# Sixty-four attention heads on four engines: paired low parts, an earlier scaling, a subtraction moved to GpSimd, and a cell layer with six output banks

## What is computed

```python
y = x.reshape(b, t, 16, 8).transpose(0, 2, 1, 3)           # 16 heads of 8 features
scores = jnp.einsum('bhtk,bhsk->bhts', y, y) / math.sqrt(8)
attn = jax.nn.softmax(scores, axis=-1)
o = jnp.einsum('bhts,bsc->bhtc', attn, x)                  # values: all 128 features
return o.transpose(0, 2, 1, 3).reshape(b, t, 16 * c) @ weight
```

```python
def step(c, xt):
    ft = sigmoid(xt @ wf.T + c @ uf.T + bf); it = sigmoid(xt @ wi.T + c @ ui.T + bi)
    gt = tanh(xt @ wc.T + c @ uc.T + bc)
    return ft * c + it * gt, None
c_final, _ = lax.scan(step, c0, x)
h = tanh(einsum('tbi,oi->tbo', x, wo) + c_final @ uo.T + bo)
```

## Time and profile before

| | us |
|---|---|
| median of 3 runs | 2707.84 |
| profiled execution: its own time | 2715.62 |
| profiled execution: span | 2713.8 |
| head attention with its normalisation | about 612 to 1652 |
| cell0 and cell1, outputs only | about 2307 to 2319, and 2697 to 2711 |

### The profile page before, as it was taken

How to read it: one execution, slowest core, us unless ns; L and a number is a source line. 1 busy time by engine, 2 the same in 40 slices (tenths; PEclk the granted TensorE clock), 3 DMA queues, 4 the chain that set the end, 5 groups by cost and what they waited for, 6 DMA issues and landing times. The chain is left out here.

```text
span 2713.8 us, 34921 instructions
## 1 busy us (share of the span) xinstructions
PE 2542.2 (94%) x11075; PEld 1905.0 (70%) x11075; DVE 2209.5 (81%) x3128; ACT 1828.7 (67%) x3038; POOL 1227.6 (45%) x1258
## 2 busy tenths in 40 slices
PE   7899999996999999999999998899999999788888
PEld 4788888874666666666666665688888886467656
DVE  6687777777999999999999996787778875577665
ACT  4455555556888888888888885455555555566676
POOL 3566766664233233232332322466766663154411
PEclk9999999998999999999999999999999999788999
DMA  4566666644333333333333331566666650000000
GB/s 110 116 143 138 136 137 145 144 98 160 101 104 99 106 102 98 109 101 102 103 102 105 102 91 44 125 144 142 136 137 145 143 120 8 24 24 8 9 7 33
DMA packets 107384, 271.46 MB, mean 100 GB/s; under 512 B 30784, under 2 KB 35648, under 8 KB 107072
## 3 DMA queue, kind: packets, MB, share of 16 engines
q1 hardware_dynamic: 82192, 235.42, 35.4%
q0 software_dynamic: 24576, 33.62, 4.6%
q10 hardware_dynamic: 432, 0.20, 0.0%
HBM read 258.35 MB, written 10.76 MB: 99 GB/s over the span
## 5 line engine op out<-in xcount | busy, mean ns | idle before, releaser
L684 POOL TENSOR_TENSOR moe_experts_lo<-moe_experts_hidden,moe_experts_hi 128x512 fp32r<-128x512 f32 x512 | 662.4, 1294 | 340.5 <-ACT moe_experts_hi L622 340.3
L968 DVE TENSOR_TENSOR heads_e_lo<-heads_e,heads_e_hi 128x1024 fp32r<-128x1024 f32 x512 | 616.1, 1224 | 25.9
L629 ACT ACTIVATE psum<-psum 128x512 f32<-128x512 f32 x512 | 298.0, 582 | 478.6 <-PE psum L90 478.6
L802 POOL DMA_DIRECT2D heads_left<-heads_parts x512 | 307.5, 616 | 671.5 <-PE psum L856 610.3
L908 ACT ACTIVATE heads_e<-psum 128x1024 f32<-128x1024 f32 x512 | 520.8, 1024 | 108.0 <-PE psum L856 108.0
L656 DVE TENSOR_TENSOR moe_experts_weighted<-moe_spread,psum 128x512 f32<-128x512 f32 x512 | 351.3, 686 | 189.4 <-PE psum L90 185.7
L88 PE MATMUL psum<-heads_e_hi,heads_v_lo 128*128 128x512 f32 x1024 | 429.6, 420 | 18.3 <-DVE heads_u L934 18.3
L88 PE MATMUL psum<-moe_n_hi,moe_w_lo 128*128 128x512 f32 x1024 | 400.8, 391 | 5.6 <-PEq L54 5.4
L89 PE MATMUL psum<-heads_e_lo,heads_v_hi 128*128 128x512 f32 x1024 | 404.2, 395 | 0.0
L90 PE MATMUL psum<-heads_e_hi,heads_v_hi 128*128 128x512 f32 x1024 | 400.7, 391 | 0.0
L89 PE MATMUL psum<-moe_n_lo,moe_w_hi 128*128 128x512 f32 x1024 | 400.0, 391 | 0.0
(11 more groups left out here) (403 smaller groups left out, 4078.1 us busy)
## 6 DMA issues: line engine op xcount, KB each, us to landing
moe_spread<-moe_mask SPq DMA_DIRECT2D x128, 1024.0 KB, 10.2
heads_right<-heads_parts SPq DMA_DIRECT2D x512, 64.0 KB
heads_left<-heads_parts POOLq DMA_DIRECT2D x512, 64.0 KB, 2.5
heads_scale<-heads_inverse_copy SPq DMA_DIRECT2D x64, 512.0 KB, 3.7
moe_experts_raw<-in_gate SPq DMA_DIRECT2D x16, 256.0 KB, 11.7
moe_experts_raw<-in_up SPq DMA_DIRECT2D x16, 256.0 KB, 11.8
moe_experts_raw<-in_down SPq DMA_DIRECT2D x16, 256.0 KB, 11.7
heads_parts<-heads_e_hi SPq DMA_DIRECT2D x16, 256.0 KB, 3.2
```

The source lines that it names most:

```text
L629: act.activation(psum[:, GATE + p % 2, :], psum[:, GATE + p % 2, :], ACT.Silu).then_inc(silu_ready, 1)
L684: pool.tensor_tensor(lo[:, p, :], hidden[:, p % 2, :], f(hi[:, p, :]), ALU.subtract).then_inc(low_ready, 1)
L802: eng.dma_start(f(tile[row:row + 2 * HEAD, h % 2, :]), parts_dram[dims, order:order + 2, at]).then_inc(loaded[h % 2], 16)
L968: dve.tensor_tensor(e_lo[:, s, :], e[:, s % 4, :], f(e_hi[:, s, :]), ALU.subtract).then_inc(low, 1)
```

## The change

- **Low parts in pairs.** VectorE goes in steps of two key tiles: cast of the even tile, then one subtraction 128x2048 for both tiles, once both high parts are there. `low` counts pairs, and so do the waits of ScalarE (ring buffer free) and TensorE.
- **Scaling earlier.** `scale_sums` goes after the cast of tile 4 and ahead of the low parts of tiles 4 and 5 (before: after the low part of tile 5).
- **`invert` later.** It goes behind the cast of tile 0 (before: ahead of it).
- **`u_lows` on GpSimd**, ahead of the `heads_left` loads of three heads on.
- **Cells.** The eight outputs take turns in six banks, four of which hold gate sums until the last step's gates are taken; the `wo` products run four outputs ahead of the `uo` products.

```diff
@@ head_attention, gpsimd
+                def u_lows(g):
+                    for half in range(HALVES):
+                        pool.wait_ge(u_high, g * HALVES + half + 1)
+                        pool.tensor_tensor(u_lo[:, g % 2, half, :], u[:, half, :], f(u_hi[:, g % 2, half, :]),
+                                           ALU.subtract).then_inc(u_low, 1)
                 for h in range(2, COUNT):
+                    if h >= 3:
+                        u_lows(h - 3)
                     pool.wait_ge(scores_done, (h - 1) * TILES)
                     load_head(pool, left, (0, 0), h, left_loaded)
+                for g in range(COUNT - 3, COUNT):
+                    u_lows(g)
@@ tensor, scalar
-                    pe.wait_ge(low, h * TILES + s + 1)
+                    pe.wait_ge(low, (h * TILES + s) // 2 + 1)
-                    after(act, low, n - 3)
+                    after(act, low, n // 2 - 1)
@@ vector
-                for n in range(COUNT * TILES):
+                for n in range(0, COUNT * TILES, 2):
                     h, s = n // TILES, n % TILES
+                    dve.wait_ge(exp_done, n + 1)
+                    after(dve, out_done, n - (TILES - 1))
...
+                    dve.tensor_copy(e_hi[:, s, :], e[:, s % 4, :]).then_inc(dve_high, 1)
                     if s == 0 and h >= 1:
                         invert(h - 1)
...
-                    dve.tensor_tensor(e_lo[:, s, :], e[:, s % 4, :], f(e_hi[:, s, :]), ALU.subtract).then_inc(low, 1)
-                    if s == TRAIL - 1 and h >= 1:
+                    if s == 4 and h >= 1:
                         scale_sums(h - 1)
-                    if s == TILES - 1 and h >= 1:
-                        u_lows(h - 1)
+                    dve.wait_ge(dve_high, n // 2 + 1)
+                    dve.wait_ge(act_high, n // 2 + 1)
+                    dve.tensor_tensor(e_lo[:, s:s + 2, :], e[:, s % 4:s % 4 + 2, :], f(e_hi[:, s:s + 2, :]),
+                                      ALU.subtract).then_inc(low, 1)
...
-                u_lows(COUNT - 1)
@@ recurrent_layer
-        OUT = 2
+        OUTS = (2, 3, 6, 7, 4, 5)
...
+                def output_from_input(n):
+                    at, bank = slice(n * BANK, (n + 1) * BANK), OUTS[n % len(OUTS)]
+                    for half in range(HALVES):
+                        if bank in SUMS[half]:
+                            pe.wait_ge(gates_ready, (BATCH - 1) * (3 * HALVES) + half * 3 + SUMS[half].index(bank) + 1)
+                    after(pe, h_ready, n - len(OUTS) + 1)
+                    product(pe, psum[:, bank, :], w["wo"], (n_hi[:, at], n_lo[:, at]), last=False)
+                AHEAD = 4
+                for n in range(AHEAD):
+                    output_from_input(n)
                 for n in range(BATCH * HALVES):
...
+                    product(pe, psum[:, OUTS[n % len(OUTS)], :], w["uo"], (c_hi[:, half, :], c_lo[:, half, :]),
                             first=False).then_inc(out_ready, 1)
+                    if n + AHEAD < BATCH * HALVES:
+                        output_from_input(n + AHEAD)
```

More of the change, by code:

```diff
@@ L781, in head_attention @@
         VALUE_BANKS = TOKENS // BANK
-        def highs(h, s):
-            by_act = sum(i in ACT_HIGH for i in range(s + 1))
-            return h * len(ACT_HIGH) + by_act, h * (TILES - len(ACT_HIGH)) + (s + 1 - by_act)
         def turned_value(k):
@@ L935, in scale_sums @@
                                           psum[:, OUT + half, :], ALU.mult).then_inc(scaled_ready, 1)
[L937 to L941, removed]
                 def add_batch(b):
@@ L953, in _ @@
                     dve.tensor_copy(turned_value(k), psum[:, k % 8, :]).then_inc(v_by_dve, 1)
-                for n in range(COUNT * TILES):
+                for n in range(0, COUNT * TILES, 2):
                     h, s = n // TILES, n % TILES
+                    dve.wait_ge(exp_done, n + 1)
+                    after(dve, out_done, n - (TILES - 1))
+                    if n < BATCH:
+                        dve.wait_ge(copied[n], BATCH_COPIED)
+                    dve.tensor_copy(e_hi[:, s, :], e[:, s % 4, :]).then_inc(dve_high, 1)
                     if s == 0 and h >= 1:
                         invert(h - 1)
[L958 to L967, removed]
-                    dve.tensor_tensor(e_lo[:, s, :], e[:, s % 4, :], f(e_hi[:, s, :]), ALU.subtract).then_inc(low, 1)
-                    if s == TRAIL - 1 and h >= 1:
-                        scale_sums(h - 1)
-                    if s == TILES - 1 and h >= 1:
-                        u_lows(h - 1)
-                    if s == 3 and h > HEADS and h % HEADS == 2:
+                    if s == 4 and h >= 1:
+                        scale_sums(h - 1)
+                    dve.wait_ge(dve_high, n // 2 + 1)
+                    dve.wait_ge(act_high, n // 2 + 1)
+                    dve.tensor_tensor(e_lo[:, s:s + 2, :], e[:, s % 4:s % 4 + 2, :], f(e_hi[:, s:s + 2, :]),
+                                      ALU.subtract).then_inc(low, 1)
+                    if s == 2 and h > HEADS and h % HEADS == 2:
                         add_batch(h // HEADS - 1)
@@ L1045, in _ @@
                 from_cell(BATCH - 1)
+                def output_from_input(n):
[8 more added lines that the diff above has]
+                    output_from_input(n)
                 for n in range(BATCH * HALVES):
-                    half, bank, at = n % HALVES, OUT + n % 2, slice(n * BANK, (n + 1) * BANK)
-                    after(pe, h_ready, n - 1)
-                    product(pe, psum[:, bank, :], w["wo"], (n_hi[:, at], n_lo[:, at]), last=False)
+                    half = n % HALVES
                     if n < HALVES:
                         pe.wait_ge(low_ready, BATCH * HALVES + half + 1)
-                    product(pe, psum[:, bank, :], w["uo"], (c_hi[:, half, :], c_lo[:, half, :]),
+                    product(pe, psum[:, OUTS[n % len(OUTS)], :], w["uo"], (c_hi[:, half, :], c_lo[:, half, :]),
                             first=False).then_inc(out_ready, 1)
+                    if n + AHEAD < BATCH * HALVES:
+                        output_from_input(n + AHEAD)
             @block.scalar
@@ L1070, in _ @@
                     after(act, added, n - 1)
-                    act.activation(h[:, n % 2, :], psum[:, OUT + n % 2, :], ACT.Tanh, bias=columns["bo"]).then_inc(h_ready, 1)
+                    act.activation(h[:, n % 2, :], psum[:, OUTS[n % len(OUTS)], :], ACT.Tanh, bias=columns["bo"]).then_inc(h_ready, 1)
             @block.vector
```

## The result

The changed kernel takes **2755.41 us** (median of 4 runs, 2750.14 to 2770.1) where the kernel before takes 2707.25 on the same chip: ratio 1.0191, 95% interval 1.0173 to 1.0209. It is slower, as forecast (2723), but by 48 us instead of 15, and 3 us outside the range. The profiled execution took 2750.14, its span 2748.4, against 2715.62 and 2713.8 before.

The account below looks back on a forecast made before the run. TensorE, with one hole per head, bounded the old kernel; the scaling-to-scaling loop would bind next. 15.49 + 0.35 = 15.84 us a head against 15.51: heads +20, ends 0, cells -5, so +15 on 2707.84: 2723 us, range 2692 to 2752.

Parts of the forecast that it names:

- The exclusion between VectorE and GpSimd: `u_lows` on GpSimd: each half shuts VectorE out for about 1.0 to 1.1 us, in place of 0.60 each.
- The inverse loop binds: From scaling over `invert` and SyncE's small DMAs back to scaling: 15.49 us, as long as the head was.
- The loads beside the small DMAs: GpSimd's delayed `heads_left` loads lie across SyncE's DMA chain: 0.35 us a head, between 0 and about 4.
- One loop where there are two: The prediction summed only the scaling-to-scaling loop, 15.49 us; `heads_right` loads following `heads_scale` gave its lower price of 0.
- Early scaling removes the 0.47: Scaling ahead of the low parts of tiles 4 and 5 ends TensorE's 0.47 us stall per head; at most 30 us.
- Pairs, 0.24 us a head saved, "hidden by some 4 us": Paired low parts save VectorE 0.24 us a head; the later first tile is hidden, TensorE being six tiles behind.
- The sum: Heads +20, ends of the stage 0, cells -5: +15 us, giving 2730.6 against the profiled 2715.62.
- the start: Second head of the stage, with no `add_head` to cover the wait of 1.8 us: about -1 us.
- the end of the stage: Behind the last head GpSimd's two halves take 2 x 1.27 instead of 1.20 on the path: +1.3 us.
- Cells: Three more `wo` products in TensorE's idle time: about 2.7 us gained per cell layer, 5.4 together, between 3.5 and 6.6.
- loads hurt much: Rival: loads cost 1.0 us a head in place of 0.35, a head takes 16.5, the whole 2763; chance 0.12.

Follow-up runs that it names:

- e2: Changed kernel with `invert` ahead of the cast of tile 0 again, nothing else: 2707.39 us, ratio 0.9984 to the kernel before.
- e1: Changed kernel with GpSimd's eight `heads_left` loads ahead of its two `u_lows` subtractions: 2745.85 us, ratio 1.0127 to the kernel before.
- e6: Changed kernel with `heads_left` loads ahead of GpSimd's subtractions and `heads_right` loads ahead of SyncE's wait for the inverse: 2746.95 us, ratio 1.0127 to the kernel before.
- e5: Changed kernel with the eight `heads_right` loads ahead of SyncE's wait for the inverse: 2743.48 us, ratio 1.0124 to the kernel before.
- e4: Changed kernel with `u_lows` back on VectorE and `invert` ahead of the cast of tile 0: 2688.02 us, ratio 0.9906 to the kernel before.
- e7: Changed kernel with `u_lows` back on VectorE, `invert` ahead of tile 0's cast, `heads_right` loads ahead of SyncE's inverse wait: 2670.91 us, ratio 0.9847 to the kernel before.
- e3: Changed kernel with `u_lows` back on VectorE, behind the last pair of a head: 2704.08 us, ratio 0.9973 to the kernel before.
- e11: Kernel before with only `scale_sums` moved, between the cast and the low part of tile 4: 2687.79 us, ratio 0.9911.
- e13: Kernel before with early scaling, `heads_right` loads ahead of SyncE's inverse wait and the cells' part, low parts single: 2672.74 us, ratio 0.987.
- e12: Kernel before with only low parts in pairs, scaling behind the pair of tiles 4 and 5: 2784.85 us, ratio 1.0254.
- e10: Kernel before with only `u_lows` moved to GpSimd, ahead of the `heads_left` loads: 2713.13 us, ratio 1.0002.

## Why the prediction was right in sign and wrong in size

- *The exclusion between VectorE and GpSimd:* right. It was to cost about 1.0 to 1.1 for each half; the cast grew by 1.07 and the pair by 0.99. Scaling to reciprocal was to be 9.04 and is 8.95. The time that VectorE gave up it did not keep.
- *The inverse loop binds:* right. The scaling waits for the landing of `heads_scale` 60 times, 1.2 us each. e2, which takes a cast out of the loop, shortened the head by 0.61.
- *The loads beside the small DMAs:* **this term was mis-sized**, at 0.35 a head where the runs show 0.71. The step was "I take 0.35 a head, near the lower end, because half of the 64 landings are at 3.7 or below beside such loads". Those landings are of `heads_scale` with the right loads issued behind it, and the left loads are issued ahead of the small DMAs. The landing of `heads_scale` did stay at 3.6, but the four small DMAs ahead of it, of 1 KB each, paid: their wait on SyncE went from 0.98 to 107.3 / 64 = 1.68, and small to spread from 2.37 to 3.08. With the left loads out of their way it is 2.3 again (e1, e6). Another 0.10 is the sum's own, which took 1.29 + 0.98 = 2.27 for a stretch that is 2.37 from start to start. In all that gives 15.49 - 0.09 - 0.02 + 0.81 + 0.08 = 16.27, and the measured period is 16.28. Against the forecast's 15.84 it is 0.44 more, 28 us over 63 heads, of which the loads are 0.36.
- *One loop where there are two:* the prediction called the right loads unimportant, as they follow `heads_scale` at once. It never walked SyncE's queue past them to the scores step. Beyond the first loop this one cost 0.2 a head (e5), so the sum hardly suffered; but it kept e4 at 15.20 until the right loads were moved (e7, 15.01), and e3 met it in 33 heads.
- *Early scaling removes the 0.47:* right, 0.34 in the mean and 0.44 in the median head (e11), and all of it with the right loads moved (e7, e13).
- *Pairs, 0.24 us a head saved, "hidden by some 4 us":* right for the change as a whole, and by luck. TensorE's low parts are hidden; what else stands behind the pair on VectorE is not, and in the change only the early scaling keeps the 1.1 us of e12 away.
- *The sum:* made against the profiled execution it gave 2730.6, and that took 2750.14. The heads took 50.4 more where the sum had 20 (30 of it unforeseen: 28 from the period, the rest from counting 61 heads from 15.51 where 63 go from 15.48); the start -3.1 for -1, the end of the stage +2.5 for +1.3 (605.0 for 602.6 from the last scaling to the last `moe` matmul), the rest of the program -15.3 for -5.4, of which the outputs are 6.9. 30.4 - 2.1 + 1.2 - 9.9 = 19.6. The medians differ by more (48 for 15) because the profiled execution of the changed kernel was its fastest of four, and the one of before lies 8 us above its median.
- *Cells:* right. 3.4 and 3.5 where 2.7 was taken between 1.75 and 3.3: the pace behind the shorter idle time was kept in full (2.04 + 1.3 = 3.34).

The rival "loads hurt much" (1.0 a head, 2763) was nearer than the forecast; it had 0.12.

## What to carry to other kernels

When work is moved between engines, first ask which loops of semaphores the moved instructions stand in, then walk each loop through every queue, past the DMAs issued behind the one that matters, until it comes back to its start: here 0.2 us of reciprocal behind a cast was worth 38 us between two profiled executions and 56 in the medians. Price contention from a row of the same kind of transfer in the same order: a large DMA that lands unharmed with loads issued behind it says nothing of a chain of tiny ones with loads ahead, nor of itself with loads beside it (4.8 for 3.7 in e10). And work with two inputs in SBUF that is moved from a nearly full VectorE to GpSimd need not be time that VectorE gets back: here it cost VectorE 1.07 + 0.99 for 1.20. Test each part of a change alone: here the pairs cost 71 us, the early scaling gained 26, the moved subtraction 0 and the cells 8, and with the right loads moved as well the change without its two harmful moves is 1.5% faster than the kernel before.

## What was not expected of the hardware

- *Who wins the shared port.* The prediction's row had one operation of each kind; the Trainium skill (SBUF — State Buffer, "Who interferes with whom") says that the loser waits for the whole instruction, and the traces agree: 1.07 and 0.99 for a half of 1.27. But two GpSimd instructions in a row can pass before VectorE gets its turn: casts of 3.21 (0.69 alone) and pairs of 5.35 (2.29 alone), though the VectorE record begins up to 0.63 us before GpSimd's. In the changed kernel they mostly took turns (1.76, then 3.27, GpSimd's halves 3.51 together). What decides it was not tried, nor why the pair at 1221.06 was shut out while GpSimd was, by the record, still issuing its last load.
- *Who pays for loads beside it depends on the order.* From the first of four 1 KB DMAs to their last completion and the next issue it is 3.08 us with the left loads issued just ahead, 2.3 without, and 2.36 in e10, where the left loads start 0.7 behind the first of the four. The 0.5 MB of `heads_scale` land in 3.6 or 3.7 with loads issued behind them and in 4.8 with left loads beside them (e10). In e7 and e13, whose right loads are issued ahead of the small DMAs, these take 2.84 and 2.71. What in the queues makes the difference was not tried.
